# Score products from rounded parts, kept weight parts, three slots of turned probabilities

## The reference, cut to what matters

```
proj = layernorm(x) @ W_qkv                # 32 query heads, 8 key/value heads, 64 wide
q, k = rope(q), rope(k)
attn = q . k / 8                           # float32
attn = where((q_pos >= k_pos) & (q_pos < k_pos + 64), -inf, attn)   # a band is masked out
w = softmax([attn, sink])[..., :-1]
x = x + (w @ v) @ W_out
```

## Time and profile before

| | |
|---|---|
| three runs | 1068.28, 1069.7, 1072.6 us; median 1069.7 |
| span of the profiled execution (the run's own time is not listed apart) | 1063.8 us |
| TensorE busy | 1032.3 us, 97% |
| VectorE busy | 918.9 us, 86% |
| ScalarE, GpSimd busy | 653.7 us, 663.4 us |
| granted TensorE clock, mean | 0.993 of full |
| attention | to about 800 us of the span; then the experts |

### The profile page before, as it was taken

How to read it: one execution, slowest core, us unless ns; L and a number is a source line. 1 busy time by engine, 2 the same in 40 slices (tenths; PEclk the granted TensorE clock), 3 DMA queues, 4 the chain that set the end, 5 groups by cost and what they waited for, 6 DMA issues and landing times.

```text
span 1063.8 us, 32339 instructions
## 1 busy us (share of the span) xinstructions
PE 1032.3 (97%) x13013; PEld 729.8 (69%) x13013; DVE 918.9 (86%) x1962; ACT 653.7 (61%) x1670; POOL 663.4 (62%) x607
## 2 busy tenths in 40 slices
PE   6899999999999999999999999999998999999996
PEld 4466666666666666666666666666566999999995
DVE  6999999999999999999999999999966777677773
ACT  4676667666667666667776656777654455544451
POOL 5657776767666888666777877667762422233332
PEclk8999999999999999999999999999999999999998
DMA  3544555544333344333343344333324344454421
GB/s 94 150 114 117 129 135 130 137 118 131 95 84 81 95 110 105 97 100 79 80 111 101 95 131 111 94 86 98 100 80 159 87 121 121 126 125 124 101 44 21
DMA packets 115574, 112.11 MB, mean 105 GB/s; under 512 B 35264, under 2 KB 103936, under 8 KB 115296
## 3 DMA queue, kind: packets, MB, share of 16 engines
q1 hardware_dynamic: 97648, 90.29, 31.3%
q0 software_dynamic: 7296, 8.55, 5.0%
q10 hardware_dynamic: 10480, 11.20, 3.8%
HBM read 74.84 MB, written 21.83 MB: 91 GB/s over the span
## 4 chain that ended last, share of the span: by engine, by line
PE 60%; DVE 35%; issue 2%; ACT 1%; DMA 0%; SPq 0%; POOLq 0%; DVEq 0%
PE bank L1536 21%; DVE probs_ring L1124 15%; DVE probs_t L1133 13%; PE bank L1701 11%; PE bank L1512 11%; PE bank L1712 7%; DVE heads_sb L1153 4%; PE bank L1715 4%; PE bank L1568 1%; PE bank L1441 1%; PE bank L1676 1%; PE bank L1458 1%; PE bank L1476 1%; PE bank L1596 1%; DVE neg_max L1124 0%
## 5 line engine op out<-in xcount | busy, mean ns | idle before, releaser
L841 ACT ACTIVATE probs_ring<-probs_ring,neg_max 128x512 f32<-128x512 f32 x512 | 365.9, 717 | 210.2 <-DVE neg_max L1124 209.4
L1124 DVE CUSTOM_DVE_ANT_0 probs_ring<-bank,mask,sink_neg 128x512 f32<-128x512 f32 x512 | 360.3, 738 | 24.9 <-PE bank L1512 23.8
L1133 DVE STREAM_TRANSPOSE probs_t<-probs_ring 128x1024 f32<-128x1024 f32 x256 | 317.8, 1241 | 0.2 <-ACT probs_ring L841 0.2
L1512 PE MATMUL bank<-qk_st 64*128 64x512 f32 x1024 | 280.6, 624 | 11.6 <-DVE neg_max L1124 7.4
L1536 PE MATMUL bank<-probs_t,v_quads 32*64 32x256 f32 x8192 | 247.9, 381 | 0.0
L1536 PEld LDWEIGHTS bank<-probs_t,v_quads 32*64 32x64 f32 x8192 | 179.3, 132 | 75.4 <-issue 48.1
L670 POOL TENSOR_TENSOR chunk_sb<-chunk_sb,rope_sb 128x512 f32<-128x512 f32 (+1 forms) x94 | 119.8, 1275 | 111.1 <-issue 80.6
L789 POOL DMA_INDIRECT out<-expert_sb,slots x40 | 77.8, 1945 | 150.6 <-DVE expert_sb L1385 143.3
L1512 PEld LDWEIGHTS bank<-qk_st 64*128 64x128 f32 x1024 | 85.3, 185 | 77.0 <-DVE neg_max L1124 41.5
L1043 ACT ACTIVATE hidden<-bank,b_sb 128x320 f32<-128x320 f32 x128 | 60.5, 524 | 107.1 <-PE bank L1701 107.1
L675 POOL TENSOR_TENSOR qk_st<-chunk_sb,swap_sb 128x512 f32<-128x512 f32 (+1 forms) x94 | 120.0, 1276 | 7.4
(11 more groups left out here) (189 smaller groups left out, 1352.5 us busy)
## 6 DMA issues: line engine op xcount, KB each, us to landing
v_quads<-v_rows SPq DMA_DIRECT2D x128, 128.0 KB
recip_wide<-recip_rows SPq DMA_DIRECT2D x64, 256.0 KB
w_raw<-in_L_ffn_w SPq DMA_DIRECT2D x14, 1024.0 KB, 8.2
swap_sb<-chunk_sb SPq DMA_DIRECT2D x314, 32.0 KB
w_raw<-in_L_attn_W_qkv SPq DMA_DIRECT2D x32, 256.0 KB, 2.9
slots<-slot_rows SPq DMA_DIRECT2D x9, 662.5 KB, 4.0
slot_rows<-x2T ACTq DMA_DIRECT2D x8, 662.5 KB, 6.2
w_raw<-in_L_attn_W_qkv SPq DMA_DIRECT2D x64, 64.0 KB, 2.7
```

The lines of the kernel that those rows point to most:

```text
L841: nc.scalar.activation(probs[(g * UNITS + n) % RING][:, :], probs[(g * UNITS + n) % RING][:, :], ACT.Exp, bias=neg_max[j][:, n:n + 1], sca ...
L1124: nc.vector.tensor_tensor_reduce(probs[(g * UNITS + n) % RING][:, :], SCORE[SCORE_OF[n // 2][n % 2]][:, :], mask[:, L - P - t * P:2 * L - ...
L1133: nc.vector.transpose(probs_t[j][:, :, (h // 2) * (2 * P):(h // 2 + 1) * (2 * P)] .rearrange("p b (h q) -> p h b q", h=2)[:, :, :, t * BLK ...
L1512: nc.tensor.matmul(SCORE[SCORE_OF[n // 2][hh]][:, :], qk_st[j][half, h // 2, t * P:(t + 1) * P], qk_st[j][half, PAIRS, :], start=True, sto ...
```

## The change

- The rotated q and k are split like the projection's operands. The rotation writes back into `chunk_sb`; ScalarE makes the rounded part (`qk_high`, steps 3 for Q23, -9 for KV and -6 for Q01, so steps 3, 7 and 10 of a period) and GpSimd the rest (`qk_low`, steps 3, 6 and 10). A score pair becomes three pairs of float32r products. Group 0 keeps float32 (`qk_first`).
- `k_twice` copies both parts of k and waits for the low one; SyncE issues it last in the period.
- The parts of the weights of the first batch's 8 groups are written to memory (`keep_w`); later batches load them back (`load_w_again`, issued just ahead of `k_twice`) and are not split again. ScalarE, not GpSimd, makes the high part in the first batch; the split moves from step 1 to step 13.
- `probs_t` is one tensor of three slots, one for each pair of heads in turn; a new wait of VectorE at unit 8 is for P.V of the group before.
- The residual addition moves from step 38 to 43.

```diff
-        qk_st = [sb("qk_st0", [P, PAIRS + 1, L], c=actx)]
+        qk = [sb("qk0", [P, 2, PAIRS + 1, L], F32R, c=actx)]
-        probs_t = [sb(f"probs_t{i}", [P, BLOCKS, UNITS * BLK], c=actx) for i in range(2)]
+        probs_t = sb("probs_t", [P, SLOTS, BLOCKS, 2 * P], c=actx)
-        SPLIT_AT, SECOND_SPLIT_AT = -15, -10
+        QK_HI_AT, QK_LO_AT = {3: Q23, -9: KV, -6: Q01}, {3: Q23, -10: KV, -6: Q01}
+        W_HI_AT, SPLIT_AT, SECOND_SPLIT_AT = -7, -3, -10
-        Y_FIRST_OUT_AT, Y_OUT_AT, RESIDUAL_AT = 30, 31, 38
+        Y_FIRST_OUT_AT, Y_OUT_AT, RESIDUAL_AT = 30, 31, 43
...
             def k_twice(g, j):
-                sp.wait_ge(s_rot, g * CHUNKS + 1)
-                sp.dma_start(qk_st[j][HD:P, PAIRS, :], qk_st[j][0:HD, PAIRS, :]).then_inc(s_k_twice, 16)
+                sp.wait_ge(s_qk_lo, rotated(g * CHUNKS + KV))
+                sp.dma_start(qk[j][HD:P, :, PAIRS, :].bitcast(F32), qk[j][0:HD, :, PAIRS, :].bitcast(F32)).then_inc(s_k_twice, 16)
+            def keep_w(g, j):
+                sp.wait_ge(s_w_lo, g + 1)
+                for part, w in enumerate((w_hi, w_lo)):
+                    sp.dma_start(w_parts[g, part], w[j][:, :, :].rearrange("p c n -> p (c n)").bitcast(F32)).then_inc(s_w_kept[j], 16)
+            def load_w_again(g, j):
+                sp.wait_ge(s_w_kept[j], NKV * 16)
+                sp.wait_ge(s_proj, (g - 1) * CHUNKS)
+                for part, w in enumerate((w_hi, w_lo)):
+                    sp.dma_start(w[j][:, :, :].rearrange("p c n -> p (c n)").bitcast(F32), w_parts[g % NKV, part]
+                                 ).then_inc(s_w_again[j], 16)
...
                 swap_halves(g + 1, Q01)
-                k_twice(g + 1, (g + 1) % 2)
-                if g + 3 < GROUPS:
+                if g + 1 < NKV:
+                    keep_w(g + 1, (g + 1) % 2)
+                if g + 3 < NKV:
                     load_w(g + 3, (g + 3) % 2)
                 v_out(g + 1)
                 v_in(g + 1, (g + 1) % 2)
                 swap_halves(g + 1, Q23)
+                if NKV <= g + 3 < GROUPS:
+                    load_w_again(g + 3, (g + 3) % 2)
+                k_twice(g + 1, (g + 1) % 2)
...
+            def qk_low(g, c):
+                pool.wait_ge(s_qk_hi, rotated(g * CHUNKS + c))
+                nc.gpsimd.tensor_tensor(qk_part(g, c, 1), chunk_sb[c][qk_rows(c), :], qk_part(g, c, 0).bitcast(F32),
+                                        ALU.subtract).then_inc(s_qk_lo, 1)
...
+            def qk_high(g, c):
+                act.wait_ge(s_rot, g * CHUNKS + c + 1)
+                if g > 1:
+                    act.wait_ge(s_scores, (g - 1) * UNITS)
+                nc.scalar.activation(qk_part(g, c, 0), chunk_sb[c][qk_rows(c), :], ACT.Copy).then_inc(s_qk_hi, 1)
...
+                    if u == UNITS // 2 and later(g):
+                        dve.wait_ge(s_pv, g + 1)
...
-                        pe.wait_ge(s_rot, g * CHUNKS + Q01 + 1)
+                        if g == 0:
+                            pe.wait_ge(s_rot, Q01 + 1)
+                        else:
+                            pe.wait_ge(s_qk_lo, rotated(g * CHUNKS + Q01))
                         pe.wait_ge(s_k_twice, g * 16 + 16)
...
+                        for m, (q_part, k_part) in enumerate([(0, 0), (1, 0), (0, 1)]):
+                            for half, out_bank in zip(halves, outs):
+                                ins = nc.tensor.matmul(out_bank, qk[j][half, q_part, h // 2, t * P:(t + 1) * P],
+                                                       qk[j][half, k_part, PAIRS, :], start=(m == 0), stop=(m == 2))
+                                if m == 2:
+                                    ins.then_inc(s_scores, 1)
```

More of the change, by code:

```diff
@@ L133, in moe_layer @@
         s_w_lo = sem("s_w_lo")
+        s_w_kept = [sem(f"s_w_kept{i}") for i in range(2)]
+        s_w_again = [sem(f"s_w_again{i}") for i in range(2)]
         s_v_out = sem("s_v_out")
@@ L452, in slot_bank, with qk_rows, qk_part, pair_slot @@
             return SCORE[c] if e == 0 else banks[c]
+        def qk_rows(c):
+            return slice(0, HD) if c == KV else slice(0, P)
+        def qk_part(g, c, part):
+            return qk[g % 2][qk_rows(c), part, PAIRS if c == KV else c - Q01, :]
+        def pair_slot(g, pair):
+            return (g * PAIRS + pair) % SLOTS
+        def rotated(q):
+            return q - CHUNKS + 1
         def chunk_cols(c):
@@ L662, in rotate @@
                 q = g * CHUNKS + c
-                rows = slice(0, HD) if c == KV else slice(0, P)
+                rows = qk_rows(c)
                 pool.wait_ge(s_chunk_out, q + 1)
                 pool.wait_ge(s_swapped[c], g * 32 if c == KV else g * 64 if c == Q01 else (g + 1) * 64)
-                if c == KV and g > 1:
-                    pool.wait_ge(s_scores, (g - 1) * UNITS)
                 straight, swapped = chunk_sb[c][rows, :], swap_sb[c][rows, :]
@@ L674, in rotate @@
                     pool.wait_ge(s_rot, Q23)
[L675 removed]
+                nc.gpsimd.tensor_tensor(qk_first[:, c - Q01, :] if g == 0 else straight, straight, swapped,
                                         ALU.add).then_inc(s_rot, 1)
+            def qk_low(g, c):
+                pool.wait_ge(s_qk_hi, rotated(g * CHUNKS + c))
+                nc.gpsimd.tensor_tensor(qk_part(g, c, 1), chunk_sb[c][qk_rows(c), :], qk_part(g, c, 0).bitcast(F32),
+                                        ALU.subtract).then_inc(s_qk_lo, 1)
             pool.wait_ge(s_small_in, 16)
@@ L682, in pool_step @@
                     rotate(g, j, c)
-                if n == (SECOND_SPLIT_AT if g == 1 else SPLIT_AT) and 0 < g < GROUPS - 1:
+                if n in QK_LO_AT and g > 0:
+                    qk_low(g, QK_LO_AT[n])
+                if n == (SECOND_SPLIT_AT if g == 1 else SPLIT_AT) and 0 < g < NKV - 1:
                     split(g + 1, 1 - j, (g + 1) // 2)
@@ L843, in act_step @@
                                          accum_out=sums[j][:, n:n + 1]).then_inc(s_probs, 1)
+                if n in QK_HI_AT and g > 0:
+                    qk_high(g, QK_HI_AT[n])
+                if n == (SECOND_SPLIT_AT if g == 1 else W_HI_AT) and 0 < g < NKV - 1:
+                    w_high(1 - j, (g + 1) // 2, g + 1)
                 if n == Y_FIRST_OUT_AT and g < GROUPS - 1:
@@ L861, in act_step, with w_high @@
                     nc.scalar.activation(sink_exp[:, :], sink_arg[:, :], ACT.Exp).then_inc(s_sink_exp, 1)
-            def w_high(j):
-                act.wait_ge(s_w_in[j], 48)
+            def w_high(j, half, g):
+                act.wait_ge(s_w_in[j], half * 48 + 48)
+                if later(g - 1):
+                    act.wait_ge(s_proj, (g - 1) * CHUNKS)
+                    act.wait_ge(s_w_kept[j], g // 2 * 32)
                 nc.scalar.activation(w_hi[j][:, :, :], w_raw[j][:, :, :], ACT.Copy).then_inc(s_w_hi, 1)
```

58 lines of the change are left out of this document (36 added, 22 removed).

## The result

| | before | after |
|---|---|---|
| median us (runs) | 1071.15 (4) | 1335.22 (4) |
| lowest to highest | 1068.28 to 1072.93 | 1330.84 to 1339.57 |
| span of the profiled execution | 1063.8 | 1331.2 |
| mean granted clock | 0.993 | 0.905 |

A forecast was written before the change was run, and what follows sets the result against it. TensorE and VectorE were taken as nearly level before, K's late copy as deciding after. 24 x (30.5 - 23.6) = 166 and 7 x (28.1 - 23.9) = 29 give +195; 1063.8 + 195 + 5.9 = 1265 us, range 1165 to 1320.

The forecast's parts named there:

- What bounds it, and the sign: K's copy, issued last by SyncE, would hold each next period's first score: +195 us, slower with chance 0.92.
- K's rotation: On GpSimd, unchanged, ending 15.7 us into the period; ScalarE's rounding of K waits for it.
- V behind ScalarE's wait: K's rounding on ScalarE stands ahead of units 8, 9 and V's copy: V ready at 18.1 us, against 16.0.
- Rival C: ScalarE's wait doesn't delay V, so Q23's swaps end at 22.85 us: 1184 or 1153 us, chance 0.14.
- The swaps of Q23: On SyncE, behind V's reads, taking 2.45 us and ending 24.95 us into the period.
- the landing of the copy: K's copy queues behind 786 KB of weight parts: 4.35 us, 0.7 more for the copy, landing at 30.0 us.
- The other seven periods: Periods without reloaded weight parts would take 28.1 us instead of 23.9, +29 us together.
- The clock: TensorE at half clock after each stall: first score 0.7 us longer, 0.18 saved, +0.5 us a period.
- D: TensorE's clock costs its upper bound, 1.2 us more in 31 periods: 1302 us, chance 0.10.
- B: K's copy does not queue behind the weight parts; only their two issues come before it: 1233 us, chance 0.18.
- E: K's copy lands before TensorE wants it and the cheaper scores show: 1030 to 1050 us, chance 0.05.
- F: Rounded products cost what float32 did, or gains just pay small waits, copy in time: about 1070 us, chance 0.03.

The follow-up runs named there:

- run 3: Changed kernel with the kept weight parts loaded one period later, right behind the swaps of Q01, none ahead of K's copy: 1238.5 us, 1.1644 of before.
- run 7: Changed kernel with parts loaded behind Q01's swaps, K's rounded part after V's copy, K's copy between V's reads and Q23's swaps: 1125.1 us, 1.0506 of before.
- Run 2: Changed kernel, but ScalarE makes K's rounded part behind units 8, 9 and the copy of V: 1301.8 us, 1.2239 of before.
- Run 1: Changed kernel, but the copy of K is issued ahead of the two transfers of kept weight parts: 1246.2 us, 1.1716 of before.
- run 12: Kernel before with the kept weight parts alone, reloaded behind Q01's swaps; float32 scores and K's copy as they were: 1078.4 us, 1.0113 of before.
- run 5: Changed kernel with four unused products (fewer up to g = 6) on TensorE ahead of its wait for K's copy: 1319.4 us, 1.2375 of before.
- run 9: As run 8, with one product of rounded parts per score instead of three: 1116.3 us, 1.0424 of before.
- run 8: Changed kernel, K's swap ahead of the reciprocals' spread, K's low part before Q01's, K's copy ahead of V's write, parts early: 1119.3 us, 1.0448 of before.
- run 6: Changed kernel, but K's copy is issued behind Q01's swaps as before the change; parts stay at the end: 1258.5 us, 1.1752 of before.

## Why the prediction fell short

- **What bounds it, and the sign: right.** The copy of K became the last thing before each first score. Moving the parts alone took back 87 of 264 us (run 3), moving parts, copy and K's rounded part 209 (run 7).
- **K's rotation: right.** Forecast to end 15.7 + 0.5 us in, 16.6 on the mean; the reciprocals go out at 4.65 (forecast 4.6).
- **V behind ScalarE's wait: right in kind, 1 us short.** Forecast 18.6, 19.6 on the mean. In the period above ScalarE waits 3.07 us for the rotation of K, then come the rounding, units 8 and 9, and V:

```profile
527.87 0.63 ACT L886 ACTIVATE qk<-chunk_sb 64x512 fp32r<-64x512 f32 x1 [3.07 <-POOL chunk_sb L714]
528.41 0.71 ACT L895 ACTIVATE probs_ring<-probs_ring,neg_max 128x512 f32<-128x512 f32 x1
...
529.82 0.36 ACT L879 ACTIVATE v_next<-bank 128x256 f32<-128x256 f32 x1
```

  These lengths are the forecast's; here V is ready 19.5 us in, because the rotation ended at 527.84, 17.1 in. Rival C falls. Its sum also left out the clock's 0.5 us a period, so by my own terms V's delay was priced at 65 us, not 81. Run 2, with V at 17.5 us in the mean (C had 16.0), gains only 24: Q23's chunk, which I had put near 21.5, came at 22.9 there and at 23.9 in the kernel after.
- **The swaps of Q23**: forecast to end 25.45 in, 26.8 on the mean, 32 us over 24 periods. Half of it is in four of them: in g = 10, 13, 18 and 26 the swaps end 30.2 us in, in the other twenty 26.1. In three of the four it is the wait for x2T, which I had not seen behind ScalarE's new wait; in g = 13 it is VectorE's, told at the end.
- **The step that failed: the landing of the copy.** I gave 24.95 + 5.05, so 5.05 us from the end of the swaps to the next first score. It is 33.4 - 26.8 = 6.6: 1.2 of issuing the parts (I had 1.1 in the rival only, since I took the parts as moving meanwhile), then 5.4 from the copy's issue. 1.55 us x 24 = 37 us. My price for 786 KB came from 662.5 KB in 4.0 us; that it was too low because V's reads and the swaps are still on the queue is likely, not tested. Run 1 measures issuing and queueing together: 3.3 us a period, where the forecast's difference between periods with and without parts was 2.4.
- **The other seven periods** cost 41 us instead of 29. I costed keeping the parts at nothing, and run 12 gives 12 us for it in the kernel before; that these are the same 12 isn't shown. In g = 1 to 4 the swaps end at 24.5 to 25.7 us (forecast 25.45), and the first score comes 3.2 to 4.9 us after the copy's issue, where I had 2.65.
- **The base.** I took 23.6 us for the later periods from one quoted period; their mean is 24.12. That makes my sum 12 us too large, and hides as much of the miss. VectorE's idle time, my bound on what cheaper scores could bring, is 33.5 / 600 x 725 = 40 us, not 42; the forecast doesn't use it.
- **In numbers:** 24 x (33.38 - 30.5) = 69, less 24 x 0.52 = 12, and 41 - 29 = 12 for the other periods: 69 of the 68 us between 263 and 195.
- **The clock: right in kind.** Half clock at the start of each period as forecast; run 5, which gives part of it back, gains some 9 us, where I had 0.5 x 31 = 16 for all of it. D's 1302 would have needed 1.2 more a period, with K's chunk and what follows late as well; the reciprocals go out only 0.6 us later than before (4.65 against 4.06), so D falls, though its number is the nearest to the result; the half clock of P.V in g = 10 (2.6 us) is a cost of the clock that no sum of mine held.
- **B** falls by runs 1 and 3. **E and F** fall on the copy, and more than I thought: by run 9 cheaper scores bring nothing even with the copy in time.

**What stays open.** The profiled execution of run 8 has a span 53 us over that of before. Its periods g = 0 to 7 hold 19 us of this, where run 12 has 12 for keeping the parts; the four long periods hold 22 (23.8 to 23.9 us each before), which are the work of the run's own swap; the eighteen other periods up to g = 29 hold 5, 0.3 us each; what follows g = 29 holds 9, and the first score comes 2 us sooner than before. Whether an order without those long periods would come near the time of before, and what part the three slots of turned probabilities have, wasn't tried.

## What to carry to other kernels

A copy that the next period's first instruction needs must not be the last item of a queue's list, and least of all stand behind a bulk load on the same queue: place bulk loads by what comes behind them, also across the turn of the loop, as run 6 shows. A new wait on an engine that works in order also delays what else stands behind it, as x2T shows: list that too. Price such a chain over many periods rather than one, with a transfer's landing as it is behind the traffic that is really ahead of it. And though TensorE was 99% busy, cheaper work on it was worth nothing here, where a round trip through three engines and a queue is nearly as long as the period.

## What the hardware showed besides

In the kernel after, three small operations of VectorE for the expert layer, which read two tensors in SBUF, took far longer than the usual 0.17 to 0.19 us (L398 at 535.99 in the kernel before, with GpSimd idle). Each of the three runs four times in the kernel; this is the first time, and the others took the usual time. VectorE's timeline, and then GpSimd's:

```profile
455.00 1.08 DVE L1377 TENSOR_TENSOR full<-slot_f,slot_end 128x8 f32<-128x8 f32 x1
456.12 1.20 DVE L1378 SCALAR_TENSOR_TENSOR scatter_idx<-full,slot_f 128x8 uint32<-128x8 f32 x1
...
457.65 3.49 DVE L406 TENSOR_TENSOR xn<-gates,top_sum 128x32 f32<-128x32 f32 x1
```

```profile
454.79 1.27 POOL L709 TENSOR_TENSOR chunk_sb<-chunk_sb,rope_sb 64x512 f32<-64x512 f32 x1 [1.87 <-DMA swap_sb<-chunk_sb]
456.02 1.28 POOL L710 TENSOR_TENSOR swap_sb<-swap_sb,rope_sb 64x512 f32<-64x512 f32 x1
...
459.83 1.25 POOL L710 TENSOR_TENSOR swap_sb<-swap_sb,rope_sb 128x512 f32<-128x512 f32 x1
```

VectorE's three end at 456.08, 457.32 and 461.14; GpSimd's rotations end at 456.06, 457.30 and 461.08. Each seems to have waited for GpSimd's operation to end, the last one through three of them in a row. The Trainium skill, page SBUF — State Buffer, section Who interferes with whom, says that a VectorE instruction with two inputs in SBUF and a GpSimd instruction that reads SBUF block one another for a whole instruction; these rows agree. Together they cost VectorE 5.2 us more than 0.19 us each would. This is in g = 13, and TensorE's next score (463.67) waited 3.99 us for VectorE; the period is 36.8 us long, against 33.4 in the mean.
